# A graph layer's type embedding as one product of one-hot rows, its last 128 columns in two-relation chunks, and query units moved behind the second query tile

## The chip, the cores and the metric

The kernel runs on one core of a Trainium2 chip. The metric is the device time of one execution in microseconds (us); lower is better. PE is TensorE (PEld its weight loads), DVE is VectorE, ACT is ScalarE, POOL is GpSimd, SP is the engine that issues most DMAs.

## What is computed

The input `x` has 625 nodes of 768 features; there are 10,000 edges with a relation of 0 to 2, and each node has a type of 0 to 2. Two blocks follow one another, each `x + gnn + attention`, then `x + feed-forward`. The change lies in the first block. Its graph part is three relational layers:

```python
def rgcn_conv(h, src, dst, edge_type, w_rel, w_root, bias):
    xw = einsum('nd,rde->rne', h, w_rel)
    msg = xw[edge_type, src] * inv[dst, edge_type][:, None]   # inv: 1 / edges of that relation at dst
    return segment_sum(msg, dst) + h @ w_root + bias

h = concatenate([xn, node_emb[node_type]], axis=-1)     # 768 + 128 = 896 features
h = relu(rgcn_conv(h, ..., w_rel1, w_root1, b1))        # 896 -> 896
h = relu(rgcn_conv(h, ..., w_rel2, w_root2, b2))        # 896 -> 768
h = relu(rgcn_conv(h, ..., w_rel3, w_root3, b3))        # 768 -> 768
```

`xn` is the normalised `x`; `node_emb` is 3 x 128. The attention beside it has 12 heads of 64 with 256 random features, `relu` of the features of queries and keys, and no softmax.

## The kernel before

All matrix products run on PE with operands split in two: `hi` is the value rounded to the type PE takes, `lo` the rest, and a product is hi*hi + hi*lo + lo*hi, three matmuls (`split_product`, L179; `split_product_wide`, L187, with two halves of 314 nodes as the moving side, six matmuls). The 625 nodes are five tiles (`TT`), the last of 113; 896 features are seven slabs of 128 (`K1`), 768 are six (`KD`).

**Weights** come through a ring of two slots (`Ring`, `Stream`). A chunk is up to seven slabs by 256 columns. SP loads chunk n as soon as DVE has split chunk n-2 (`load_chunk`, L102); ACT writes `hi` (`ring_high`, L128) once PE is done with chunk n-2 (`st.freed`), then DVE writes `lo` (`ring_low`, L139), and PE waits for that (`st.split`).

**The stages that matter here** run one after another, with a barrier between:

- `phase_attend` "m0", six head pairs. For a pair PE makes key features of five tiles (`features_k`, L476), four tiles of query features m = 0 to 3 (`features_q`, L502), the products of keys and values (`keys_values`, L526) and the attention output. The next pair's key and query projections are cut in 12 units of six matmuls (`project_unit`, L187), and strewn in between: one after each key tile and one more, one after each of the query tiles 0, 1 and 2, and three behind `keys_values`. ACT copies a query tile (L645), DVE writes its low part (`pq_lo`, L771); query tile m waits for `pq_lo` of tile m-2, whose PSUM banks it takes.
- `phase_project` "p0": the attention's output projection (15 tiles, L179), while DVE and ACT decode packed edge counts. Here the type embedding is made: `embedding_rows` builds one-hot rows (L1016 to L1019), `embed` multiplies by them on PE (L905), ACT and DVE write the result and its low part as `k.et`, a seventh slab beside the six of `k.xt`. Then a check of the counts (L914) and a short loop that recounts.
- `phase_rgcn` "g1", the first layer (896 to 896), and "g2". The output columns are cut by 256, with 128 left over in g1: cuts 0 to 3. A written-out list of jobs sets the order on all engines:

```python
jobs = [(kind, c, r) for c in range(len(cuts))
        for kind, r in (("Y", 0), ("Y", 1), ("G", 0), ("Y", 2), ("G", 1), ("R", 3), ("G", 2))]
```

"Y r" is h times the weights of relation r: five tiles in PSUM banks 0 to 2 in turn, 7 x 3 matmuls each; ACT (L1503) and DVE (L1536) write the two halves of `y`. Tile i waits for `y_lo` of tile i-3. "G r" multiplies `y` by the edge counts (L1479, 20 matmuls of 314 columns for 128 output columns), "R" is h times the root weights, transposed (L187, 42 matmuls of 314 for 128 output columns). DVE adds G and R up. Each job uses one chunk of weights but G, which uses none.

In g1 the reciprocals of the counts are made first: PE sums counts (`sum_counts`, L1442; relations 0 and 1 ahead of all jobs, 2 behind tile 4), and DVE runs `inverse` six times, each behind a `y_lo` (`INVERSE_AT`, tiles 0, 1, 2, 3, 6, 7; L1520, L1521, L1524, L1525). The first "G" waits until the last of them has read its sums (`sum_read`, set by L1521).

Of the kernel before, what the change touches and what calls it, by code (L numbers as in the profile page):

```python
# [6 lines left out]
F32 = mybir.dt.float32  # L7
# [10 lines left out]
P = 128  # L18
# [150 lines left out]
def rgcn_chunks(w_rel, w_root):  # L169

    d_in, d_out = w_root.shape
    return [(d_in // P, w, [(0, w, weight_view(m)[:, :, c:c + w])])
            for c, w in column_cuts(d_out) for m in (w_rel[0], w_rel[1], w_rel[2], w_root)]
# [161 lines left out]
def phase_attend(k, name, second, rf=None):  # L335
# [3 lines left out]
    with ExitStack() as ctx:  # L339
# [87 lines left out]
        def _(pe):  # L427
# [54 lines left out]
            def features_q(p):  # L482
                for m in range(4):
# [29 lines left out]
                    if m < 3:  # L513
                        project_unit(p + 1, KD + m)

# [289 lines left out]
EMBED_AT = 7  # L805
PROJ_BANKS = 4
# [3 lines left out]
def phase_project(k, name, src, dst, edge_type, node_emb, node_type):  # L810
# [13 lines left out]
    with ExitStack() as ctx:  # L824
# [25 lines left out]
        type_i = spare[0:RELS, part[6]].bitcast(I32)[:, 0:NODES]  # L850
        type_f = spare[0:RELS, part[7]][:, 0:NODES]
        onehot = spare[0:RELS, part[8]]
# [3 lines left out]
            "edges_loaded", "emb_loaded", "iota_made", "own_made", "emb_made", "emb_ready", "emb_hi", "emb_lo",  # L856
# [13 lines left out]
        def _(sp):  # L870
# [30 lines left out]
        def _(pe):  # L901
            def embed():
                pe.wait_ge(s["emb_made"], 1)
                for h in range(2):
                    mm = pe.matmul(k.pair[3][:, h, 0:HN], emb_sb[:], onehot[:, h * HN:(h + 1) * HN], start=True, stop=True)  # L905
                mm.then_inc(s["emb_ready"], 1)

            def check():
# [8 lines left out]
                pe.wait_ge(s["emb_lo"], 1)  # L917
                pe.matmul(k.banks[7][:, 0:2], k.ones[:], over[:], start=True, stop=True).then_inc(s["check_mm"], 1)

            for c in range(3):  # L920
                pe.wait_ge(*st.split(c))
                wh = st.views(c)
                for t in range(TT):
# [10 lines left out]
                    if i == EMBED_AT:  # L934
                        embed()
# [16 lines left out]
        def _(act):  # L952
# [7 lines left out]
            for t in range(TT):  # L960
# [12 lines left out]
                if t == 3:  # L973
                    act.wait_ge(s["emb_ready"], 1)
                    act.activation(halves(k.et[:, 0, 0, :]), k.pair[3][:, :, 0:HN], ACT.Copy).then_inc(s["emb_hi"], 1)
# [3 lines left out]
        def _(dve):  # L979
# [77 lines left out]
            dve.memset(quot[:, 0, 0:P], 1.0).then_inc(s["ones_f"], 1)  # L1057
            dve.memset(shift[:], -(BASE / 2 - 1) / BASE).then_inc(s["shift_made"], 1)
# [5 lines left out]
            for i in range(3 * TT):  # L1064
# [10 lines left out]
                if i == EMBED_AT - 3:  # L1075
                    embedding_rows()
# [297 lines left out]

RECOUNT = 2
STEPS = RELS * ET // RECOUNT


def phase_rgcn(k, name, h_in, h_out, d_in, d_out, bias, layer):
# [5 lines left out]
    cuts = column_cuts(d_out)  # L1385
    with ExitStack() as ctx:  # L1386
# [9 lines left out]
            "sum_mm", "sum_read"))  # L1396
# [4 lines left out]
        jobs = [(kind, c, r) for c in range(len(cuts))  # L1401
# [1643 lines left out]
```

## Time and profile before

| | us |
|---|---|
| median of 3 runs (lowest, highest) | 2229.34 (2228.92, 2235.43) |
| the profiled execution | 2230.74 |
| its span, first to last instruction | 2229.0 |

| stage | from, to in the span (us) |
|---|---|
| attention m0, from its first product | 62.4 to 261.4 |
| projection p0 | 261.4 to 316.3 |
| first relational layer g1 | 316.3 to 579.1 |
| second and third layer | 579.1 to 981.7 |
| feed-forward, second block | 981.7 to 2229.0 |

PE is busy for 91% of the span. In the timeline a row is one instruction, or some like ones in a run; its length of 0.28 us for a matmul is that from first column in to last out, and the pace is the distance of two starts. In brackets stands how long the engine was idle, and who ended that.

### The profile page before, as it was taken

What the parts mean: (1) busy time and instruction counts of PE and PEld (TensorE: products, weight loads), DVE (VectorE), ACT (ScalarE), POOL (GpSimd) and SP (SyncE); (2) the same over time, 40 slices, a digit from 0 to 9 for tenths busy, and PEclk for the clock granted to TensorE, in tenths of its full rate; (3) what the DMA queues carried; (4) which work ended last, traced back from release to release, by engine and by line L of the source; (5) the groups of instructions that cost most, each with busy time, mean ns of one, the idle gap of its engine ahead of it and who ended that gap; (6) DMA issues with size and microseconds to landing.
All of it is one profiled execution on the core that took longest, in us unless ns stands there. A gap on an engine that the chain in (4) does not pass through costs nothing. (4 is left out here: it accounts for less than half of the span.)

```text
span 2229.0 us, 34175 instructions
## 1 busy us (share of the span) xinstructions
PE 2031.5 (91%) x13715; PEld 1919.2 (86%) x13715; DVE 1324.0 (59%) x1860; ACT 940.3 (42%) x1143; POOL 89.9 (4%) x70
## 2 busy tenths in 40 slices
PE   5899889999999999955899979799979999999996
PEld 4889779999999999955789879699968888888885
DVE  8455665333334343446456756553358888888886
ACT  6444411221211122111356633222247777777775
POOL 0000000000000000000001100000000100101001
PEclk9999989999999999977899978899989999999998
DMA  3311134211111121110210030412269999999997
GB/s 81 101 29 29 57 100 93 67 34 51 51 58 58 29 73 49 58 29 1 93 29 29 15 135 15 158 48 93 79 233 385 384 384 378 366 372 374 367 374 269
DMA packets 186156, 313.71 MB, mean 141 GB/s; under 512 B 12641, under 2 KB 86884, under 8 KB 185628
## 3 DMA queue, kind: packets, MB, share of 16 engines
q1 hardware_dynamic: 180956, 295.38, 38.0%
q0 software_dynamic: 4816, 16.62, 3.2%
q8 instruction: 88, 1.44, 0.3%
q14 instruction: 24, 0.20, 0.0%
q10 hardware_dynamic: 272, 0.07, 0.0%
HBM read 293.56 MB, written 20.40 MB: 141 GB/s over the span
## 5 line engine op out<-in xcount | busy, mean ns | idle before, releaser
L179 PE MATMUL psum<-re_whi,xt_sb 128*128 128x512 f32 (+1 forms) x1680 | 507.5, 377 | 1.5 <-DVE xt_sb L2794 1.5
L179 PE MATMUL psum<-ring_hi,xt_sb 128*128 128x256 f32 (+3 forms) x1980 | 369.1, 284 | 10.8 <-DVE m_v L694 3.9
L179 PEld LDWEIGHTS psum<-re_whi,xt_sb 128*128 128x128 f32 x1680 | 313.0, 189 | 47.0 <-issue 1.9
L2778 DVE TENSOR_TENSOR re_wlo<-moe_raw,re_whi 128x1536 fp32r<-128x1536 f32 x173 | 303.5, 1756 | 35.1 <-ACT re_whi L2732 34.4
L179 PEld LDWEIGHTS psum<-ring_hi,xt_sb 128*128 128x128 f32 (+1 forms) x1980 | 312.0, 190 | 12.0 <-issue 5.3
L179 PE MATMUL psum<-re_wlo,xt_sb 128*128 128x512 f32 (+1 forms) x840 | 313.2, 373 | 0.0
L2732 ACT ACTIVATE re_whi<-moe_raw 128x1536 fp32r<-128x1536 f32 x174 | 258.7, 1490 | 90.7 <-PE psum L179 86.7
L179 PE MATMUL psum<-ring_lo,xt_sb 128*128 128x256 f32 (+3 forms) x990 | 280.5, 283 | 0.0
L179 PEld LDWEIGHTS psum<-ring_lo,xt_sb 128*128 128x128 f32 (+1 forms) x990 | 188.1, 190 | 0.0
L179 PEld LDWEIGHTS psum<-re_wlo,xt_sb 128*128 128x128 f32 x840 | 158.9, 189 | 22.1
L128 ACT ACTIVATE ring_hi<-ring_raw 128x1536 fp32r<-128x1536 f32 (+2 forms) x67 | 102.2, 1526 | 159.8 <-PE psum L187 81.3
L2778 DVE TENSOR_TENSOR re_wlo<-re_more,re_whi 128x1536 fp32r<-128x1536 f32 x84 | 147.6, 1758 | 29.7 <-ACT re_whi L2732 29.7
L179 PE MATMUL psum<-ring_hi,gnn_sb 128*128 128x256 f32 (+1 forms) x810 | 150.1, 286 | 6.9 <-PEq L1386 4.2
L139 DVE TENSOR_TENSOR ring_lo<-ring_raw,ring_hi 128x1536 fp32r<-128x1536 f32 (+2 forms) x67 | 121.5, 1813 | 56.2 <-ACT ring_hi L128 56.0
L2732 ACT ACTIVATE re_whi<-re_more 128x1536 fp32r<-128x1536 f32 x84 | 125.2, 1490 | 41.4 <-PE psum L179 37.6
L1536 DVE TENSOR_TENSOR g_y<-psum,g_y 128x256 fp32r<-128x256 f32 (+3 forms) x105 | 42.4, 405 | 168.7 <-ACT g_y L1503 168.5
L187 PE MATMUL psum<-xt_sb,ring_hi 128*128 128x314 f32 x744 | 140.2, 310 | 0.0
L1503 ACT ACTIVATE g_y<-psum 128x256 fp32r<-128x256 f32 (+3 forms) x105 | 38.7, 369 | 232.9 <-PE psum L179 232.9
L179 PEld LDWEIGHTS psum<-ring_hi,gnn_sb 128*128 128x128 f32 (+1 forms) x810 | 127.5, 190 | 8.1 <-issue 7.8
L1479 PE MATMUL psum<-gnn_sb,g_y 128*128 128x314 f32 (+1 forms) x780 | 117.1, 308 | 0.0
L187 PEld LDWEIGHTS psum<-xt_sb,ring_hi 128*128 128x128 f32 x744 | 115.7, 191 | 0.0
L179 PE MATMUL psum<-ring_lo,gnn_sb 128*128 128x256 f32 (+1 forms) x405 | 115.6, 285 | 0.0
(400 smaller groups left out, 3288.5 us busy)
## 6 DMA issues: line engine op xcount, KB each, us to landing
moe_raw<-in_L_ffn_Wg_r SPq DMA_DIRECT2D x74, 768.0 KB, 9.0
moe_raw<-in_L_ffn_Wu_r SPq DMA_DIRECT2D x58, 768.0 KB, 8.4
moe_raw<-in_L_ffn_Wd_r SPq DMA_DIRECT2D x42, 768.0 KB, 6.2
re_more<-in_L_ffn_Wd_r SPq DMA_DIRECT2D x42, 768.0 KB, 9.4
re_more<-in_L_ffn_Wu_r SPq DMA_DIRECT2D x30, 768.0 KB, 7.8
ring_raw<-in_L_gnn_w_rel SPq DMA_DIRECT2D x18, 896.0 KB, 5.1
re_more<-in_L_ffn_Wg_r SPq DMA_DIRECT2D x15, 768.0 KB, 7.3
ring_raw<-in_L_mix_W_qkv SPq DMA_DIRECT2D x24, 384.0 KB, 4.4
```

The source lines that it names most:

```text
L128: act.activation(ring.hi[:, g % RING_SLOTS, 0:size], ring.raw[:, g % RING_SLOTS, 0:size], ACT.Copy).then_inc(ring.hi_done, 1)
L139: dve.tensor_tensor(lo, raw, hi.bitcast(F32), ALU.subtract).then_inc(ring.lo_done, 1)
L179: mm = pe.matmul(out, lhs[a], rhs[b], start=(first and i == 0), stop=(last and i == 2))
L187: mm = pe.matmul(bank_pair[:, h, 0:HN], lhs[a], rhs(b, h), start=(first and i == 0), stop=(last and i == 2))
L1479: mm = pe.matmul(pair[:, h, 0:HN], y[0:TS[t], v % 2, t, a, m * P:(m + 1) * P], k.C[0:TS[t], r, t, h * HN:(h + 1) * HN], start=(t == 0 and ...
L1503: act.activation(y[0:TS[t], v % 2, t, 0, 0:w], k.banks[i % 3][0:TS[t], 0:w], ACT.Copy).then_inc(s["y_hi"], 1)
L1536: dve.tensor_tensor(y[0:TS[t], v % 2, t, 1, 0:w], k.banks[i % 3][0:TS[t], 0:w], y[0:TS[t], v % 2, t, 0, 0:w].bitcast(F32), ALU.subtract).t ...
L2732: act.activation(whi[:, slot, :], raw[i % RAWS], ACT.Copy).then_inc(s["hi_done"], 1)
L2778: dve.tensor_tensor(wlo[:, i % RING, :], raw[i % RAWS], whi[:, i % RING, :].bitcast(F32), ALU.subtract)\
```

## The change

- **Embedding.** `k.et` is gone. p0 now makes `k.kind_rows` (99 used rows by 628 columns: a one-hot column of three types, four times over, at rows 0, 32, 64 and 96) and `k.emb` (the embedding turned, 128 by 35: hi in columns 0 to 2, lo in 32 to 34); the PE product `embed` is gone from it. In g1, `embed_products(n)` multiplies `k.emb` by the seventh slab of chunk n, hi and lo (two matmuls, 35 x 256, bank 3); ACT (`embed_high`) and DVE (`embed_low`) write its halves into `ew`; and each output tile gets, in place of three products with the seventh slab, one with `kind_rows` and `ew`, which waits for `ew_lo`. `embed_products` of the next chunk stands behind tile 3 of a Y job, or behind the first half of R, and waits for that chunk's split; that of chunk 0 stands ahead of everything.
- **Last cut of g1.** Its chunks are relations 0 and 1 side by side, and relation 2 beside the root. "Y 0" makes both relations' `y` at 256 columns, "Y 1" is gone, and the order is Y 0, Y 2, G 0, G 1, R, G 2. Chunks of g1: 14 for 16.
- **Attention m0.** The three query units of the next pair all stand behind query tile 1. In the second block's attention they stay.

```diff
 def rgcn_chunks(w_rel, w_root):
+    sides, chunks = (w_rel[0], w_rel[1], w_rel[2], w_root), []
+    for c, w in column_cuts(d_out):
+        for group in (sides[0:2], sides[2:4]) if w == P else [(m,) for m in sides]:
+            chunks.append((d_in // P, w * len(group),
+                           [(w * i, w * (i + 1), weight_view(m)[:, :, c:c + w]) for i, m in enumerate(group)]))
...
# features_q, phase_attend
-                    if m < 3:
+                    if second and m < 3:
                         project_unit(p + 1, KD + m)
+                    elif m == 1:
+                        for u in range(KD, KD + 3):
+                            project_unit(p + 1, u)
...
# phase_project
-            sp.dma_start(emb_sb[:], node_emb).then_inc(s["emb_loaded"], 16)
+            sp.dma_start(emb_f[:], node_emb.rearrange("r e -> e r"), allow_slow_non_contiguous=True).then_inc(s["emb_loaded"], 16)
...
-            for r in range(RELS):
-                sp.dma_start(type_i[r:r + 1, :], node_type.rearrange("(a n) -> a n", a=1)).then_inc(s["emb_loaded"], 16)
+            sp.dma_start(type_i, node_type.partition_broadcast(P)).then_inc(s["types_loaded"], 16)
...
-                    if i == EMBED_AT:
-                        embed()
...
# rgcn_plan, the order of jobs
+        order = (("Y", 0), ("Y", 2), ("G", 0), ("G", 1), ("R", 3), ("G", 2)) if w == P else \
+            (("Y", 0), ("Y", 1), ("G", 0), ("Y", 2), ("G", 1), ("R", 3), ("G", 2))
...
# phase_rgcn, tensor
+            def embed_products(n):
+                w = st.chunks[n][1]
+                pe.wait_ge(*st.split(n))
+                if n >= 1:
+                    pe.wait_ge(s["ew_lo"], n)
+                for a, v in enumerate(st.views(n)):
+                    mm = pe.matmul(k.banks[3][0:EMB_ROWS, 0:w], k.emb[:], v[:, KD, :], start=(a == 0), stop=(a == 1))
+                mm.then_inc(s["ew_mm"], 1)
...
+            if layer == 0:
+                embed_products(0)
                 sum_counts(0)
                 sum_counts(1)
...
-                        for j in range(kt):
+                        for j in range(full):
                             mm = split_product(pe, k.banks[i % 3][0:TS[t], 0:w],
...
+                        if layer == 0:
+                            pe.wait_ge(s["ew_lo"], n + 1)
+                            mm = pe.matmul(k.banks[i % 3][0:TS[t], 0:w], k.kind_rows[0:TYPE_ROWS, t * P:t * P + TS[t]],
+                                           ew[0:TYPE_ROWS, n % 2, off:off + w], start=False, stop=True)
                         mm.then_inc(s["y_mm"], 1)
+                        if t == EMBED_TILE and job in begins:
+                            embed_products(begins[job])
...
# phase_rgcn, vector
+            def embed_low(n):
+                w = st.chunks[n][1]
+                dve.wait_ge(s["ew_hi"], n + 1)
+                dve.tensor_tensor(ew[64:TYPE_ROWS, n % 2, 0:w], k.banks[3][0:EMB_ROWS, 0:w],
+                                  ew[0:EMB_ROWS, n % 2, 0:w].bitcast(F32), ALU.subtract).then_inc(s["ew_lo"], 1)
...
+            if layer == 0:
+                dve.memset(ew[:].bitcast(F32), 0.0).then_inc(s["ew_zero"], 1)
+                embed_low(0)
             ring_low(dve, st, 1)
```

`full` is 6 in g1 (7 slabs before) and stays `kt` elsewhere; `ew` has two slots of 256 columns.

The order of instructions at three places. First PE in m0, query tiles 1 to 3 of a pair that has a next one (L502, now L506, is a query tile; L187, now L191, a unit of `xt_sb`; names in brackets are the semaphores waited for). Before:

```order
L502 MATMUL psum<-m_qk,m_rf 128x314 [waits m0_pk_lo]
L502 MATMUL psum<-m_qk,m_rf 128x314 x3
L187 MATMUL psum<-xt_sb,ring_hi 128x314 x4
L187 MATMUL psum<-xt_sb,ring_lo 128x314 x2
L502 MATMUL psum<-m_qk,m_rf 128x314 [waits m0_pq_lo]
L502 MATMUL psum<-m_qk,m_rf 128x314 x3
L187 MATMUL psum<-xt_sb,ring_hi 128x314 x4
L187 MATMUL psum<-xt_sb,ring_lo 128x314 x2
L502 MATMUL psum<-m_qk,m_rf 128x314 [waits m0_pq_lo]
L502 MATMUL psum<-m_qk,m_rf 128x314 x3
L526 MATMUL psum<-m_v,m_phik 128x130 [waits m0_qk_lo,m0_pk_lo]
```

and now:

```order
L506 MATMUL psum<-m_qk,m_rf 128x314 [waits m0_pk_lo]
L506 MATMUL psum<-m_qk,m_rf 128x314 x3
L191 MATMUL psum<-xt_sb,ring_hi 128x314 x4
L191 MATMUL psum<-xt_sb,ring_lo 128x314 x2
L191 MATMUL psum<-xt_sb,ring_hi 128x314 x4
L191 MATMUL psum<-xt_sb,ring_lo 128x314 x2
L191 MATMUL psum<-xt_sb,ring_hi 128x314 x4
L191 MATMUL psum<-xt_sb,ring_lo 128x314 x2
L506 MATMUL psum<-m_qk,m_rf 128x314 [waits m0_pq_lo]
L506 MATMUL psum<-m_qk,m_rf 128x314 x3
L506 MATMUL psum<-m_qk,m_rf 128x314 [waits m0_pq_lo]
L506 MATMUL psum<-m_qk,m_rf 128x314 x3
```

Two units (12 matmuls) have moved ahead of query tile 2, and nothing stands between tiles 2 and 3 and `keys_values`.

Second PE in g1, last cut, a tile's end and the next one's start (`xt_sb` and `et_sb` are the features, `ring` the weights, `types_sb` is `kind_rows`, `emb_sb` is `k.emb`). Before, relation 0 alone:

```order
L179 MATMUL psum<-ring_lo,xt_sb 128x128
L179 MATMUL psum<-ring_hi,xt_sb 128x128
L179 MATMUL psum<-ring_hi,et_sb 128x128
L179 MATMUL psum<-ring_lo,et_sb 128x128
L179 MATMUL psum<-ring_hi,et_sb 128x128
```

and now relations 0 and 1 together, between tiles 3 and 4:

```order
L183 MATMUL psum<-ring_hi,xt_sb 128x256
L1516 MATMUL psum<-g_ew,types_sb 128x256
L1492 MATMUL psum<-ring_hi,emb_sb 35x256
L1492 MATMUL psum<-ring_lo,emb_sb 35x256
L183 MATMUL psum<-ring_hi,xt_sb 113x256
L183 MATMUL psum<-ring_lo,xt_sb 113x256
```

Three products with the seventh slab became one with the type rows, the width is 256, and two products of 35 rows for the next chunk follow.

Third DVE in g1, behind tile 3 of the first Y job (L1536, now L1625, is `y_lo`). Before:

```order
L1536 TENSOR_TENSOR g_y<-psum,g_y 128x256
L1520 TENSOR_SCALAR g_pos<-psum 128x314
L1521 TENSOR_SCALAR g_cnt<-psum 128x314
L1524 RECIPROCAL g_cnt<-g_cnt 128x314
L1525 TENSOR_TENSOR a_sb<-g_cnt,g_pos 128x314
L1536 TENSOR_TENSOR g_y<-psum,g_y 113x256
```

and now:

```order
L1625 TENSOR_TENSOR g_y<-psum,g_y 128x256
L1610 TENSOR_TENSOR g_ew<-psum,g_ew 35x256
L1600 TENSOR_SCALAR g_pos<-psum 128x314
L1601 TENSOR_SCALAR g_cnt<-psum 128x314
L1604 RECIPROCAL g_cnt<-g_cnt 128x314
L1605 TENSOR_TENSOR a_sb<-g_cnt,g_pos 128x314
L1625 TENSOR_TENSOR g_y<-psum,g_y 113x256
```

`embed_low` stands between `y_lo` of tile 3 and the fourth `inverse`, so all that follows comes after it.

## Rows read from the trace of the kernel before

**Rows 1.** The page, section 1: busy us, share of the span and instructions by engine.

```profile
PE 2031.5 (91%) x13715; PEld 1919.2 (86%) x13715; DVE 1324.0 (59%) x1860; ACT 940.3 (42%) x1143; POOL 89.9 (4%) x70
```

**Rows 2.** Busy time by engine in three stages; columns: stretch, length, PE, PEld, DVE, ACT, POOL, PEclk, DMA, GB/s.

```profile
62.38:261.39 199.01, 179.61 (x1304) 175.88 (x1305) 102.10 (x150) 83.95 (x130) 0.13 (x1) 0.97 0.16 45
261.39:316.29 54.90, 45.25 (x328) 41.40 (x328) 40.59 (x87) 15.23 (x20) 0.66 (x1) 0.90 0.26 80
316.29:579.14 262.85, 258.37 (x2005) 257.93 (x2005) 114.02 (x156) 49.14 (x84) 3.80 (x3) 0.99 0.25 68
```

**Rows 3.** The same view for four jobs of the first relational layer.

```profile
421.86:434.44 12.58, 12.58 (x108) 12.58 (x106) 2.51 (x5) 1.54 (x4) 0.00 (x0) 1.00 0.21 70
440.29:452.55 12.26, 12.26 (x87) 12.26 (x85) 2.49 (x3) 0.00 (x0) 0.00 (x0) 1.00 0.22 73
525.54:548.41 22.87, 22.87 (x212) 22.87 (x211) 7.27 (x15) 4.19 (x12) 0.00 (x0) 1.00 0.14 42
551.37:562.78 11.41, 11.41 (x108) 11.41 (x106) 1.98 (x5) 1.11 (x4) 0.00 (x0) 1.00 0.26 82
```

**Rows 4.** Timeline of PE, query features of one pair (start, length, engine, line, operation, count).

```profile
171.90 0.75 PE L187 MATMUL psum<-xt_sb,ring_hi 128*128 128x314 f32 x4
...
174.33 0.85 PE L502 MATMUL psum<-m_qk,m_rf 128*128 128x314 f32 x4 [1.38 <-DVE m_phiq L771]
...
175.88 0.75 PE L502 MATMUL psum<-m_qk,m_rf 128*128 128x314 f32 x4
176.47 0.23 PE L526 MATMUL psum<-m_v,m_phik 128*128 128x130 f32 x1
```

**Rows 5.** Timeline of DVE, the same place.

```profile
171.67 1.76 DVE L720 SCALAR_TENSOR_TENSOR m_qk<-psum,qk_bias,m_qk 64x628 fp32r<-64x628 f32 x2 [2.03 <-ACT m_qk L589]
173.46 1.53 DVE L771 SCALAR_TENSOR_TENSOR m_phiq<-psum,m_phiq 128x628 fp32r<-128x628 f32 x2
```

**Rows 6.** Timelines of DVE and PE, start of the attention output of the pair before.

```profile
157.93 0.69 DVE L791 TENSOR_TENSOR m_kv<-m_kvf,m_kv 128x512 fp32r<-128x512 f32 x1 [0.70 <-ACT m_kv L657]
...
158.72 0.51 PE L187 MATMUL psum<-m_phiq,m_kv 128*128 128x314 f32 x2
```

**Rows 7.** Timeline of PE, projection stage, around the embedding product.

```profile
280.34 1.32 PE L905 MATMUL psum<-a_sb,node_emb 3*128 3x314 f32 x4
281.59 0.39 PE L179 MATMUL psum<-ring_hi,gnn_sb 128*128 128x256 f32 x1
```

**Rows 8.** Timeline of PE, start of the first relational layer.

```profile
316.29 5.57 PE L1442 MATMUL psum<-gnn_sb,ones_r 128*128 128x314 f32 x20 [4.61 <-PEq L824]
321.66 0.41 PE L179 MATMUL psum<-ring_hi,xt_sb 128*128 128x256 f32 x1
321.87 0.41 PE L179 MATMUL psum<-ring_lo,xt_sb 128*128 128x256 f32 x1
```

**Rows 9.** Timeline of DVE, first two Y jobs of that layer.

```profile
336.93 0.42 DVE L1536 TENSOR_TENSOR g_y<-psum,g_y 128x256 fp32r<-128x256 f32 x1
337.27 0.47 DVE L1520 TENSOR_SCALAR g_pos<-psum 128x314 f32<-128x314 f32 x1
...
340.85 0.42 DVE L1536 TENSOR_TENSOR g_y<-psum,g_y 113x256 fp32r<-113x256 f32 x1
...
348.09 0.47 DVE L1521 TENSOR_SCALAR g_cnt<-psum 128x314 f32<-128x314 f32 x1
```

**Rows 10.** Timeline of PE, the same stretch.

```profile
341.33 0.39 PE L179 MATMUL psum<-ring_hi,xt_sb 128*128 128x256 f32 x1 [0.27 <-DVE g_y L1536]
...
348.88 0.60 PE L1479 MATMUL psum<-gnn_sb,g_y 128*128 128x314 f32 x3
```

**Rows 11.** Timeline of DVE, second cut, the split behind its Y 0.

```profile
405.83 2.03 DVE L139 TENSOR_TENSOR ring_lo<-ring_raw,ring_hi 128x1792 fp32r<-128x1792 f32 x1 [1.17 <-ACT ring_hi L128]
```

**Rows 12.** Timeline of PE, second cut, end of tile 3 of Y 1.

```profile
413.44 0.28 PE L179 MATMUL psum<-ring_hi,et_sb 128*128 128x256 f32 x1
413.56 0.28 PE L179 MATMUL psum<-ring_hi,xt_sb 128*113 128x256 f32 x1
```

More of the change, by code:

```diff
@@ L901, in _ @@
         def _(pe):
[L902 to L906, printed above, removed]
             def check():
@@ L1408, in phase_rgcn, with width @@
                 g_count += cuts[c][1] // P
+        y_read = {}
+        for (c, r), (v, _) in y_of.items():
+            y_read[v] = max(y_read.get(v, 0), g_at[c, r] + cuts[c][1] // P)
+            st.freed[chunk_of[c, r][0]] = (s["y_mm"], TT * (v + 1))
         for c in range(len(cuts)):
-            for r in range(RELS):
-                st.freed[4 * c + r] = (s["y_mm"], TT * (y_at[c, r] + 1))
-            st.freed[4 * c + 3] = (s["g_mm"], g_at[c, 3] + cuts[c][1] // P)
+            st.freed[chunk_of[c, RELS][0]] = (s["g_mm"], g_at[c, RELS] + cuts[c][1] // P)
+        begins, seen = {}, set()
+        for job in jobs:
+            n = chunk_of[job[1], job[2]][0]
+            if job[0] != "G" and n not in seen:
+                seen.add(n)
+                if layer == 0 and n + 1 < len(st.chunks):
+                    begins[job] = n + 1
+        ends = {chunk_of[c, r][0]: (kind, c, r) for kind, c, r in jobs if kind != "G"}
+        splits = {job: n + RING_SLOTS for n, job in ends.items() if n + RING_SLOTS <= len(st.chunks)}
         block = ctx.enter_context(k.nc.Block())
+        def width(c, r):
+            return cuts[c][1] * len(y_jobs[y_of[c, r][0]][1])
         @block.sync
@@ L1465, in _ @@
                     continue
-                for m in range(w // P):
+                for m in range(cuts[c][1] // P):
                     i = g_at[c, r] + m
@@ L1488, in _, with embed_high @@
                     mm.then_inc(s["g_mm"], 1)
+                    if kind == "R" and m == 0 and job in begins:
+                        embed_products(begins[job])
         @block.scalar
         def _(act):
+            def embed_high(n):
+                w = st.chunks[n][1]
+                if n == 0:
+                    act.wait_ge(s["ew_zero"], 1)
+                if n >= 2:
+                    act.wait_ge(*st.freed[n - 2])
+                act.wait_ge(s["ew_mm"], n + 1)
+                act.activation(ew[0:EMB_ROWS, n % 2, 0:w], k.banks[3][0:EMB_ROWS, 0:w], ACT.Copy).then_inc(s["ew_hi"], 1)
@@ L1503, in _ @@
                         act.activation(y[0:TS[t], v % 2, t, 0, 0:w], k.banks[i % 3][0:TS[t], 0:w], ACT.Copy).then_inc(s["y_hi"], 1)
-                if kind != "G" and 4 * c + r + RING_SLOTS <= len(st.chunks):
-                    ring_high(act, st, 4 * c + r + RING_SLOTS)
+                        if t == EMBED_TILE and job in begins:
+                            embed_high(begins[job])
+                elif kind == "R" and job in begins:
+                    embed_high(begins[job])
+                if job in splits:
+                    ring_high(act, st, splits[job])
                 if kind == "G" and r == 2:
-                    for m in range(w // P):
+                    for m in range(cuts[c][1] // P):
                         i = 2 * c + m
@@ L1560, in _ @@
                         dve.wait_ge(s["g_read"], i + 1)
-                    if kind == "R" and m == w // P - 1 and 4 * c + r + RING_SLOTS <= len(st.chunks):
-                        ring_low(dve, st, 4 * c + r + RING_SLOTS)
+                    if m == 0 and job in begins:
+                        embed_low(begins[job])
+                    if m == ms - 1 and job in splits:
+                        ring_low(dve, st, splits[job])
                     if kind == "G" and r == 2:
                         dve.tensor_scalar(sum_, sum_, 0.0, None, ALU.max).then_inc(s["h_f"], 1)
-                        if m == w // P - 1:
-                            for m2 in range(w // P):
+                        if m == ms - 1:
+                            for m2 in range(ms):
                                 o = 2 * c + m2
```

137 lines of the change are left out of this document (86 added, 51 removed).

## The prediction

> **What bounds the kernel now.** I read the page first: PE is busy for 2031.5 of 2229 us [rows 1]. Then the stages, where its granted clock is 0.90 to 0.99: in g1 PE is busy 258.4 of 262.9 us and DVE 114.0, so a product less is time less; m0 has 19 us of idle PE (199.0 less 179.6), and p0 some 10 [rows 2]. Then single jobs, where PE is busy end to end [rows 3]; the first two columns of such a row are all that counts here, since its product count also takes in neighbours at the edges (105, 84, 210 for two jobs in one, and 105 are theirs by the code). Last the timelines at the three places whose order changes. All of the change lies before 579 us; what follows it is the same program, and I count it as unchanged.
>
> **Pace of PE.** A Y job of 256 columns is 105 products in 12.58 us, 0.120 us each; R is 84 of 314 columns in 12.26 us, 0.146 each; at 128 columns 210 take 22.87 us and 105 take 11.41, 0.109 each [rows 3]. So a product of half the width costs nine tenths of a whole one. The Trainium skill ("TensorE: Matmul & The Clock Gate", section "Back-to-back issue gap") speaks against the merged cut: it has 81 ns for a sustained product of 128 columns, and N/2.4 + 2.5 ns, 109 ns at 256, for a single one. By that the merged job would save 210 x 0.081 - 95 x 0.109 = 6.7 us in place of the 11.5 below, as an estimate from that page; the rows have 0.109 and 0.120, and I go by them.
>
> **Attention m0.** Now query tile 2 waits for DVE: PE idles 1.38 us until `pq_lo` of tile 0 [rows 4], since DVE first writes the low part of the next keys (L720 from 171.67) and then that of tile 0 from 173.46, two of them in 1.53 us, so the first is done near 174.27 [rows 5]. That time does not hang on where query units stand. Tile 2 starts at 174.33, one unit and tile 3 follow at 175.88, `keys_values` at 176.47 [rows 4]. With all three units behind tile 1, PE still waits for the same low part, but has 0.87 us less to do behind it: 1.55 us without a start (172.78, which is 171.90 + 6 x 0.146, to 174.33) become about 0.7, and tile 3 starts once tile 2 is through and the second low part is there, both near 175.05. So `keys_values` starts 0.82 us earlier. Behind it the attention output waits for a chain of ACT and DVE that begins at the end of `keys_values` and moves with it; in the pair before, its last step ends at 158.62, and the output starts at 158.72, behind 18 products of units [rows 6]. Five pairs have a next one: 5 x 0.82 = **-4.1 us**. Bounds: 0, should that chain come out late by as much, and -6.9, all of 5 x 1.38.
>
> **Projection p0.** `embed` goes: four PE records from 280.34 to the next product at 281.59 [rows 7], **-1.25 us**. DVE loses a memset, and a low part of 628 columns shrinks to three; it gains a few operations of one to three columns ahead of its first low part, which waits for ACT anyway. Bounds: 0 (DVE's decoding sets the time of the check instead) and -1.5. The turned embedding comes by 384 packets of four bytes and the types by 320 KB in place of 7.5; both are wanted 7 us or more behind their issue, so I cost them at nothing. If either were late, DVE's decoding and with it the check would be late.
>
> **g1, up to the first G.** Here the gain is lost. PE gets 2 products first, at the low clock that stands behind the barrier (sum products 0.27 us apart in the row: 5.37 us for 20; the first Y products 0.21) [rows 8]: +0.5 us. Its tile 0 then ends about when it does now, since it has two products less. From there DVE sets the pace: a `y_lo` and an `inverse` take 3.9 us, from 336.93 to 340.85 [rows 9], for each of the first four tiles, where a tile of PE is 2.5 (12.58 / 5 [rows 3]) and will be 2.3. Already now tile 7 starts only at 341.33, released by DVE, and G 0 starts at 348.88 [rows 10] while the last L1521, on which it depends, runs from 348.09 for 0.47 us, to 348.56 [rows 9]. So PE has 0.3 us to spare there and would be 1.4 us ahead after the change. But DVE gets `embed_low` before the fourth `inverse`: near 0.35 us (a 256-column subtract is 0.42 and the next starts 0.34 on [rows 9]), and its chain starts 0.1 us later. L1521 ends near 349.0, and G 0 starts near 349.1: **+0.2 us** where the products alone would give -1.4. PE then waits in tile 5 for `ew_lo` (some 0.5 us) and before tile 7 (about 1.5 us for 0.43 now). Bounds: -1.4, and +2.5 (below).
>
> **g1, the rest.** Seven more full-width Y jobs lose 10 products each (21 to 19 a tile, five tiles): 7 x 10 x 0.120 = **-8.4 us**. R loses 4 of 42 for each 128 columns, seven times: 28 x 0.146 = **-4.1 us**. The last cut's Y jobs are 22.87 + 11.41 = 34.28 us [rows 3] and become 95 products of 256, 95 x 0.120 = 11.4, and 95 of 128, 95 x 0.109 = 10.3: **-12.6 us**. Eleven embedding steps remain behind the first G, two products each: 22 x 0.120 = **+2.6 us**; I take the 256-column pace for them and for the kind product, although one has 35 output rows and the other 99 input rows, since no row shows such shapes; bounds are 0.109 and 0.146, which is -0.2 to +0.6 us for the 22 and -0.4 to +1.0 for the 40 kind products of 256 columns behind the first G. The chain from product to `ew_lo` is about 0.4 + 0.4 us of ACT and DVE and some 0.3 between; the next chunk's first kind product comes at least one tile and 18 products later (over 4 us), so it is hidden. The split is now wanted earlier: in Y 1 behind tile 3 and not, as for its first use now, behind a G. In the second cut the split for it ends at 407.86 [rows 11], while tile 3 ends at 413.56 [rows 12], or 1.0 us less when tiles are shorter: 4.7 us of slack, and the loads are issued a whole job ahead. Every other chunk has a G or half an R more.
>
> **Sum.** -4.1 - 1.25 + 0.2 - 8.4 - 4.1 - 12.6 + 2.6 = **-27.65 us**. Against the profiled execution, 2230.74 (its span of 2229.0 and 1.7 around it, which I leave as it is), that is 2203.1; against the median of the three runs, which is 1.4 us lower, **2201.7**. A difference of 0.3%, 6.7 us, is about what a measurement of this kernel can tell from none.
>
> **Rivals.**
> 1. *m0 gives nothing.* The chain behind `keys_values` (ACT's copy, DVE's sum, ACT, DVE) competes with the ring split that DVE and ACT run there, and the attention output waits as long as it gained. For it: the margin is 0.1 us [rows 6]. Against: the split starts behind the last query tile and moves along. Then 2205.8.
> 2. *A bubble at each kind product.* It waits for `ew_lo` in the middle of a tile, and its weight load can't run ahead. The Trainium skill ("TensorE: Matmul & The Clock Gate", "Architectural detail: the array is 16× 32×32, not 1× 128×128") says that PE's queue pulls weight loads ahead of products in flight; it doesn't say that a wait hinders that. There are 55 + 7 such waits; at 0.11 us each (a product's spacing) they cost 6.8 us: 2208.5. Against it: the first product of tile 4 also stands behind a wait, and follows the last of tile 3 by 0.12 us like any other [rows 12].
> 3. *The clock falls in g1's first cut.* PE idles 1.5 us there, in place of 0.4. In m0 idle times of 1.38 us leave the clock at full speed in the stage's mean of 0.97 [rows 2, 4]. Should it fall, products at 0.21 us and not 0.12 for 3 us cost some 2 us: 2204; this is the +2.5 bound.
> 4. *Slower: splits too late.* If each embedding step waited for its chunk's split, PE would stand still in order. To lose 27.65 us over 13 steps it takes 2.1 us each, hence, with the slack of 4.7, splits 6.8 us later than now. Should they be 10 us later, the price is 13 x 5.3 = 69 less 27.65: 2270. Nothing in the rows points that way, since a split is 2.03 us on DVE [rows 11].
> 5. *It doesn't do what it says,* the removed products being hidden behind something: excluded by PE's 258.4 of 262.9 us [rows 2] for g1, but for its first cut, as costed.
>
> **Chances.** The forecast, within about 2.5 us of the sum: 0.66. Rival 1 in whole or half: 0.14. Rival 2: 0.07. Rival 3: 0.06. Rival 4: 0.02. No change, by a mix: 0.01. More gain than forecast (m0's bound, a quicker start of g1): 0.04. Rivals 1 and 3 are inside the range, and most of rival 2; the range is 2197 to 2209. Faster by over 0.3%: 0.97; within: 0.01; slower: 0.02.
>
> **What would show it.** m0: idle time before query tile 2 near 0.6 us and 24.0 us a pair (24.8 now); else that step is wrong. p0: no L905-like product and the stage 1.2 us shorter. g1: G 0 starts 32.8 us behind the stage's first product (now 348.88 - 316.29 = 32.6); PE idle before tile 7 near 1.5 us; a full-width Y job 11.4 us, and 0.24 more with its embedding step; R 11.1 us; last cut's Y jobs 11.4 and 10.3 us; the stage near 240.6 us for 262.9. Idle time of PE before L1516, beyond tile 5 of the first cut, or before L1492 would prove the hidden chain wrong, and a changed stage behind g1 would prove wrong that the rest stays as it is.

## The result, and the profile after

The changed kernel takes 2202.76 us, the median of four runs (2194.82 to 2204.11), against 2230.61 for four of the kernel before: a ratio of 0.9864 with a 95% interval of 0.9836 to 0.9893, 27.85 us less. The forecast was 2201.7 us against the median before, and 2203.1 for the profiled execution, which took 2203.24 us with a span of 2201.5. Whether the terms held is a question of its own. The page's first section, where PE has 24.9 us less than in [rows 1]:

```profile
PE 2006.6 (91%) x13496; PEld 1892.4 (86%) x13496; DVE 1327.5 (60%) x1873; ACT 942.4 (43%) x1150; POOL 90.6 (4%) x70
```

The window view of the changed kernel for m0, p0 and g1 (columns as in [rows 2]):

```profile
61.95:259.03 197.08, 182.46 (x1305) 177.92 (x1305) 101.73 (x153) 83.94 (x130) 0.14 (x1) 0.96 0.16 45
259.03:313.73 54.70, 45.06 (x323) 42.12 (x324) 40.02 (x89) 14.60 (x19) 0.67 (x1) 0.87 0.28 85
313.73:552.10 238.37, 232.32 (x1790) 231.16 (x1790) 119.21 (x164) 52.38 (x91) 3.80 (x3) 0.99 0.28 75
```

Against [rows 2] m0 is 1.9 us shorter (4.1 was forecast), p0 0.2 (1.25) and g1 24.5 (22.3). So the sum hit, and three terms missed. The same view for four jobs of g1 that answer to [rows 3]: Y 1 of the third cut, its R with an embedding step, and the last cut's two Y jobs (the first with its step):

```profile
457.71:468.92 11.21, 11.21 (x98) 11.20 (x97) 4.48 (x7) 3.76 (x7) 0.00 (x0) 1.00 0.30 83
494.46:505.79 11.33, 11.33 (x81) 11.29 (x79) 2.93 (x5) 0.38 (x1) 0.00 (x0) 1.00 0.23 76
511.64:523.07 11.43, 11.43 (x99) 11.41 (x98) 5.87 (x11) 3.18 (x7) 0.00 (x0) 1.00 0.23 75
523.07:533.40 10.33, 10.33 (x98) 10.33 (x96) 3.52 (x6) 3.08 (x6) 0.00 (x0) 1.00 0.00 0
```

A full-width Y job is 11.2 us for 12.4 to 12.6, R is 11.33 - 0.24 = 11.1 for 12.26, and the last cut has 11.43 - 0.24 + 10.33 = 21.5 us for 34.28: as forecast. The timeline of PE behind tile 3 of the first Y job:

```profile
326.97 0.28 PE L1516 MATMUL psum<-g_ew,types_sb 99*128 99x256 f32 x1
327.09 0.28 PE L1492 MATMUL psum<-ring_hi,emb_sb 128*35 128x256 f32 x1
327.21 0.28 PE L1492 MATMUL psum<-ring_lo,emb_sb 128*35 128x256 f32 x1
327.33 0.28 PE L183 MATMUL psum<-ring_hi,xt_sb 128*113 128x256 f32 x1
```

The product with the type rows (99 rows in; the "kind product" of the prediction), the two of the embedding step (35 out) and an ordinary one (113 out) start 0.12 us apart. There is no bubble at the wait, where `ew_lo` is there in time; rival 2 falls here.

Timeline of PE in m0, answering to [rows 4]:

```profile
172.38 0.46 PE L191 MATMUL psum<-xt_sb,ring_lo 128*128 128x314 f32 x2
173.35 1.57 PE L506 MATMUL psum<-m_qk,m_rf 128*128 128x314 f32 x8 [0.51 <-DVE m_phiq L778]
174.75 0.45 PE L533 MATMUL psum<-m_v,m_phik 128*128 128x130 f32 x3
```

Relative to the pair's first key features (161.29; 162.27 before), tile 2 starts at 12.06 us in both kernels, to the hundredth: its release by DVE doesn't hang on the units. `keys_values` starts at 13.46 for 14.20, 0.74 us earlier. Timeline of PE in g1's first cut, tile 5's last product, tile 7's first, and G 0; then DVE's `embed_low(1)` and its last read of the sums (answering to [rows 8 to 10]):

```profile
333.72 0.39 PE L1516 MATMUL psum<-g_ew,types_sb 99*128 99x256 f32 x1 [0.41 <-DVE g_ew L1610]
...
337.76 0.38 PE L183 MATMUL psum<-ring_hi,xt_sb 128*128 128x256 f32 x1 [1.40 <-DVE g_y L1625]
...
345.05 0.41 PE L1537 MATMUL psum<-gnn_sb,g_y 128*128 128x314 f32 x1
```

```profile
333.25 0.42 DVE L1610 TENSOR_TENSOR g_ew<-psum,g_ew 35x256 fp32r<-35x256 f32 x1
...
344.52 0.47 DVE L1601 TENSOR_SCALAR g_cnt<-psum 128x314 f32<-128x314 f32 x1
```

All three are the places named in the forecast, and DVE is what PE waits for: 0.41 us for `ew_lo`, 1.40 before tile 7, and G 0 0.06 us behind the last L1601 (344.52 + 0.47). But G 0 starts 31.32 us behind the stage's first product, 313.73, and not 32.8.

### The profile page after: what moved, and what is told of

Same layout as the page of the kernel before. It is cut to its first block and busy times, and to the rows that moved or that the text cites. A ratio compares the mean times of both kernels' runs of the same rounds, so it can differ in the third digit from the quotient of the medians.

```text
span 2201.5 us, 33777 instructions
## 1 busy us (share of the span) xinstructions
PE 2006.6 (91%) x13496; PEld 1892.4 (86%) x13496; DVE 1327.5 (60%) x1873; ACT 942.4 (43%) x1150; POOL 90.6 (4%) x70
## 3 DMA queue, kind: packets, MB, share of 16 engines
q8 instruction: 86, 1.41, 0.3%
## 5 line engine op out<-in xcount | busy, mean ns | idle before, releaser
L183 PE MATMUL psum<-ring_hi,xt_sb 128*128 128x256 f32 (+3 forms) x1920 | 357.5, 285 | 11.9 <-DVE m_v L701 3.9
L183 PEld LDWEIGHTS psum<-ring_hi,xt_sb 128*128 128x128 f32 (+1 forms) x1920 | 302.7, 190 | 13.1 <-issue 5.2
L183 PE MATMUL psum<-ring_lo,xt_sb 128*128 128x256 f32 (+3 forms) x960 | 272.5, 284 | 0.0
L183 PEld LDWEIGHTS psum<-ring_lo,xt_sb 128*128 128x128 f32 (+1 forms) x960 | 182.4, 190 | 0.0
L139 DVE TENSOR_TENSOR ring_lo<-ring_raw,ring_hi 128x1536 fp32r<-128x1536 f32 (+1 forms) x65 | 121.2, 1864 | 55.9 <-ACT ring_hi L128 55.8
L128 ACT ACTIVATE ring_hi<-ring_raw 128x1536 fp32r<-128x1536 f32 (+1 forms) x65 | 101.8, 1567 | 98.1 <-PE psum L183 44.5
L191 PE MATMUL psum<-xt_sb,ring_hi 128*128 128x314 f32 x744 | 139.8, 310 | 0.0
L1625 DVE TENSOR_TENSOR g_y<-psum,g_y 128x256 fp32r<-128x256 f32 (+3 forms) x100 | 41.6, 417 | 140.6 <-ACT g_y L1579 140.3
L191 PEld LDWEIGHTS psum<-xt_sb,ring_hi 128*128 128x128 f32 x744 | 115.3, 190 | 0.0
```

What stands on the lines that cost most here:

```text
L128: act.activation(ring.hi[:, g % RING_SLOTS, 0:size], ring.raw[:, g % RING_SLOTS, 0:size], ACT.Copy).then_inc(ring.hi_done, 1)
L139: dve.tensor_tensor(lo, raw, hi.bitcast(F32), ALU.subtract).then_inc(ring.lo_done, 1)
L183: mm = pe.matmul(out, lhs[a], rhs[b], start=(first and i == 0), stop=(last and i == 2))
L191: mm = pe.matmul(bank_pair[:, h, 0:HN], lhs[a], rhs(b, h), start=(first and i == 0), stop=(last and i == 2))
L1625: dve.tensor_tensor(y[0:TS[t], v % 2, t, 1, 0:w], k.banks[i % 3][0:TS[t], 0:w], y[0:TS[t], v % 2, t, 0, 0:w].bitcast(F32), ALU.subtract).t ...
```

## Experiments

Eleven runs, each beside the kernel before on the same chip (two of them repeat the changed kernel and the kernel before); "low clock" is time in which the trace's record of the granted clock has 0.5, 1.2 GHz (for a window row about twice what PEclk lacks to 1, times its length). With executions of one kernel that differ by up to 14 us, medians alone can't settle terms of 1 to 4 us, so each verdict rests on the length of the stage concerned. Ratios in brackets are to the kernel before, with the 95% interval.

**The changed kernel again.**

> The changed kernel once more, as the base for the runs beside it. Theory A (the terms of the sum are fixed costs): the stages keep their lengths of the first profile within 0.3 us: m0 196.65, p0 54.7, first relational layer 238.4. Theory B (what m0 and p0 gave was partly hidden, and the first relational layer's start partly favoured, by where the granted clock stood at 1.2 GHz): these three lengths change by 0.5 to 1.5 us between profiles of the same kernel, in step with how long the granted clock stands at 0.5 in each, while a steady pair of m0 stays at 24.08 us and the stretch behind the first G at 207.05 us. Time near 2203 under both.

2200.52 us (0.9858, 0.9835 to 0.9880). Window view: last pair of m0, p0 up to its last projection product, g1 up to G 0.

```profile
233.46:264.88 31.42, 23.62 (x103) 21.72 (x101) 9.01 (x20) 9.71 (x17) 0.14 (x1) 0.62 0.02 3
```

```profile
318.03:350.36 32.33, 30.48 (x226) 29.78 (x227) 26.32 (x36) 7.57 (x14) 3.80 (x3) 0.92 0.85 196
264.88:303.03 38.15, 38.15 (x300) 37.97 (x301) 32.61 (x67) 14.61 (x19) 0.67 (x1) 0.96 0.41 122
```

Behind G 0 the rest of g1 is 207.05 us, exactly as in the first profile, and pairs are 24.07 to 24.10. The other lengths moved as theory B says, in step with low clock, and one of them by more than its 1.5 us: m0's last pair is 31.42 us with 23.9 us of low clock, where the first profile had 25.49 with 7.3; p0's products 38.2 for 39.4, with 3.4 us of low clock for 6.3; g1 up to G 0 32.33 for 31.32, with 5.1 for 2.8. Theory A falls; theory B holds but for the size in m0.

**Only the query units.** The kernel before, with

```diff
-                    if m < 3:
+                    if second and m < 3:
                         project_unit(p + 1, KD + m)
+                    elif m == 1:
+                        for u in range(KD, KD + 3):
+                            project_unit(p + 1, u)
```

> The kernel before with the query units moved and nothing else. Theory A (DVE's low part of tile 0 is what query tile 2 waits for, and its time doesn't hang on the units): a steady pair takes 24.05 to 24.1 us for 24.8, the idle time before tile 2 is near 0.5 us for 1.38, and the kernel is 3.7 to 4.1 us faster than the kernel before. Rival (the attention output's chain of ACT and DVE comes late by as much): pairs stay at 24.8, 0 us. Rival (the gain in the changed kernel came with the rest of the change): 0 us too.

2227.19 us for 2230.76 (0.9976, 0.9963 to 0.9990), 3.6 us less by medians, 5 by the ratio. Window view, one steady pair, and g1 up to G 0:

```profile
137.03:161.09 24.06, 23.54 (x174) 23.12 (x173) 13.80 (x19) 11.93 (x18) 0.00 (x0) 1.00 0.12 33
```

```profile
314.55:346.68 32.13, 31.82 (x240) 31.61 (x241) 25.16 (x33) 6.72 (x11) 3.80 (x3) 0.92 0.88 202
```

A pair is 24.06 us (24.8 before), the five together 124.2 for 127.95. The gain is m0's own, and rival 1 of the prediction falls.

**The last cut taken apart.** The changed kernel, with

```diff
-        for group in (sides[0:2], sides[2:4]) if w == P else [(m,) for m in sides]:
+        for group in [(m,) for m in sides]:
```

and the plan of jobs to match.

> The changed kernel with the last 128 columns in four chunks of one relation each, as before, so only the merging is undone. Theory A (a product costs 0.109 us at 128 columns and 0.118 at 256, as the rows show): three Y jobs of 95 x 0.109 = 10.35 us take the place of 11.2 and 10.3, and two more embedding steps of 128 columns come: slower than the changed kernel by 9.5 + 0.4 = 9.9 us. Theory C (sustained products of 128 columns cost 0.081 us when issued without gaps, by the page named in the prediction): slower by about 5 us. Rival D (a chunk of two relations brings its own costs, such as a later split or G jobs that wait): slower by less than 9.

2207.81 us (0.9899, 0.9877 to 0.9920), 7.3 us over the changed kernel by medians, 9 by the ratios. The stretch from G 0 to the end of g1, in this kernel and in the changed one:

```profile
344.98:561.62 216.64, 212.42 (x1663) 211.97 (x1663) 94.60 (x138) 45.98 (x86) 0.00 (x0) 1.00 0.18 54
```

```profile
345.05:552.10 207.05, 202.84 (x1564) 202.37 (x1564) 92.90 (x129) 44.81 (x77) 0.00 (x0) 1.00 0.19 56
```

9.59 us: theory A. Three jobs of 95 products at 128 columns take 10.3 us each, 0.109 us a product, as the mean of four tiles of 128 rows and one of 113. The Trainium skill ("TensorE: Matmul & The Clock Gate", "Back-to-back issue gap") has 81 ns for it; in these products (fp32 data) the measurement decides against it. Timeline of PE, where shorter spacings stand, at an embedding step:

```profile
530.29 0.27 PE L1515 MATMUL psum<-g_ew,types_sb 99*128 99x128 f32 x1
530.40 0.23 PE L1491 MATMUL psum<-ring_hi,emb_sb 128*35 128x128 f32 x1
530.47 0.22 PE L1491 MATMUL psum<-ring_lo,emb_sb 128*35 128x128 f32 x1
530.53 0.26 PE L183 MATMUL psum<-ring_hi,xt_sb 128*113 128x128 f32 x1
530.63 0.26 PE L183 MATMUL psum<-ring_lo,xt_sb 128*113 128x128 f32 x1
```

Behind a product of 128 columns the next one starts after 0.06 to 0.07 us if it had 35 output rows, 0.10 if 113, 0.11 if 128. At 256 columns 35 and 128 rows cost the same 0.12.

**Only the embedding.** The changed kernel with both undone: query units strewn as before, last cut in four chunks.

> The embedding part of the change alone: type rows in place of a seventh slab, with the last cut in four chunks and the query units where they were. Theory A (the terms add): 27.85 less 3.7 for m0 and 9.9 for the merging leaves 14.2 us faster than the kernel before; by the terms of the prediction 1.25 + 8.4 + 4.1 + 1.1 (10 products of 0.109 for the 128-column Y job that the merging did not touch) + 2 x 1.1, less 0.2 and 3.0, is 13.9. Rival (a bubble of 0.11 us at each kind product, hidden in the whole by something else): about 7.

2216.81 us for 2230.78 (0.9946, 0.9929 to 0.9962): 14.0 us less by medians, 12 by the ratio. G 0 to the end of g1 is 216.64 us, as in the kernel above. The parts add (14.0 here, 3.6 of the query units and 9.6 of the merging are 27.2 us, for 27.85 of the whole), and a gain of about 7, as by the rival, is excluded.

**A product back in p0.** The changed kernel, with `emb_sb` loaded as before and, behind the eighth tile of the projection,

```diff
+            def embed():
+                pe.wait_ge(s["emb_loaded"], 32)
+                for h in range(2):
+                    pe.matmul(k.pair[3][:, h, 0:HN], emb_sb[:], k.xt[0:RELS, 0, 0, h * HN:(h + 1) * HN].bitcast(F32),
+                              start=True, stop=True)
```

> The changed kernel with a product like the removed one put back at its place in the projection stage (3 rows in, 128 out, twice 314 columns in full precision; its result is used by nobody). Theory A (the product's 1.25 us lay on PE's path, and the projection stage came out only 0.2 us shorter because its clock was low for longer): at equal time of low clock the stage's products take 1.25 us more, and the kernel is 1.2 us slower. Rival (DVE's decoding sets the end of the stage, and the product was hidden): 0 us, with idle time of PE before the check shorter by 1.25.

2200.56 us (0.9863, 0.9848 to 0.9877): in the executions' times the difference can't be seen. Timeline at the place, and the window up to the last projection product:

```profile
282.47 1.32 PE L913 MATMUL psum<-xt_sb,node_emb 3*128 3x314 f32 x4
283.73 0.38 PE L183 MATMUL psum<-ring_hi,gnn_sb 128*128 128x256 f32 x1
```

```profile
263.53:303.11 39.58, 39.58 (x305) 38.75 (x305) 32.62 (x67) 14.64 (x19) 0.67 (x1) 0.96 0.38 118
```

The record is that of [rows 7], and the stretch takes 39.58 us with 3.4 us of low clock. Sorted by low clock, the eleven profiles and the two first ones fall in place: with the product 39.55, 39.56 and 39.58 us at 3.1 to 3.4 us and 40.73 at 6.2; without it 38.11, 38.11 and 38.16 at 3.1 to 3.4, and 39.30 to 39.37 at 6.2 to 6.3. (Two more, of the kernels with fillers below, have 38.7 and 38.9 at 3.4: there the first products ran at full clock and waited for DVE.) So the product cost 1.4 us on PE's path, and 3 us more of low clock cost 1.2 and hid it in the first profile.

**The first reciprocal earlier.** The changed kernel, with

```diff
-INVERSE_AT = (0, 1, 2, 3, 6, 7)
+INVERSE_AT = (None, 0, 1, 2, 5, 6)
...
             dve.wait_ge(s["small"], 16)
+            if layer == 0:
+                inverse(0, 0)
```

> The changed kernel with the first reciprocal of the counts ahead of the first y_lo, where DVE stands idle for 2.6 us, and the others behind tiles 0, 1, 2, 5 and 6. Theory A (DVE's chain of low parts and reciprocals binds PE in the first cut): the waits in tile 5 (0.57 us over a product's spacing), before tile 7 (1.57) and before G 0 (0.17) go, 2.3 us faster than the changed kernel, and G 0 starts 2.3 us earlier behind the stage's first product. Rival (those idle times are borrowed: PE would wait later for the splits of the next chunks, for which DVE is late as well): less than 0.7 us. Slower, if tile 3 waits for a first y_lo that now comes 1 us later.

2198.08 us (0.9850, 0.9831 to 0.9869). Timeline of PE, the kind product of tile 5 and G 0:

```profile
332.66 0.39 PE L1516 MATMUL psum<-g_ew,types_sb 99*128 99x256 f32 x1 [1.31 <-DVE g_ew L1610]
...
342.10 0.60 PE L1537 MATMUL psum<-gnn_sb,g_y 128*128 128x314 f32 x3
```

G 0 comes 30.33 us behind the stage's first product (311.77), 1.0 us earlier at the same 2.8 us of low clock, not 2.3. The wait before tile 7 is gone, but tile 5 waits 1.31 us for `ew_lo`: I had put four reciprocals ahead of the low part of tile 3, where three were. DVE binds, as said; my order for it was a poor one. The last experiment has a better order.

**Low parts in halves.** The changed kernel, where `qk_high` signals behind each of its two copies in m0, and

```diff
-                dve.wait_ge(s["qk_hi"], qk_count(p, a))
                 for hd in range(2):
+                    dve.wait_ge(s["qk_hi"], 2 * qk_count(p, a) - 1 + hd)
```

(the lines for m0; in the second block's attention the one wait stays).

> The changed kernel, where in m0 DVE begins the low part of the next keys and queries behind the first of ACT's two copies and not behind both. Theory A (the rest of the wait before query tile 2 is DVE's chain behind ACT's copy of the keys, 1.57 us of ACT and 1.75 + 0.77 of DVE in a row): the chain ends 0.8 us earlier, the idle time before tile 2 (0.5 us in a pair, 0.7 start to start) goes, pairs take 23.4 us for 24.08, and the kernel is 5 x 0.67 = 3.3 us faster. Rival (keys_values, which waits for the same chain, or the attention output's chain takes the wait over): 0 to 1 us.

2191.69 us (0.9828, 0.9816 to 0.9841). Window view, one pair; timeline of PE at query tiles 2 and 3, and of DVE:

```profile
135.59:158.89 23.30, 23.30 (x174) 23.16 (x173) 13.81 (x18) 11.94 (x18) 0.00 (x0) 1.00 0.12 34
```

```profile
146.68 0.47 PE L191 MATMUL psum<-xt_sb,ring_lo 128*128 128x314 f32 x2
146.98 1.44 PE L506 MATMUL psum<-m_qk,m_rf 128*128 128x314 f32 x8
148.26 1.01 PE L533 MATMUL psum<-m_v,m_phik 128*128 128x130 f32 x8
```

```profile
144.20 1.75 DVE L732 SCALAR_TENSOR_TENSOR m_qk<-psum,qk_bias,m_qk 64x628 fp32r<-64x628 f32 x2 [1.24 <-ACT m_qk L596]
145.99 1.53 DVE L783 SCALAR_TENSOR_TENSOR m_phiq<-psum,m_phiq 128x628 fp32r<-128x628 f32 x2
```

A pair takes 23.30 us, PE is busy in all of it, and tile 2 follows the unit without a wait. DVE starts its part for the next keys 0.81 us behind ACT's start (144.20 behind 143.39), where it was 1.60. So it is in all three kernels with this edit; in the others with the moved units a pair takes 24.1. The five pairs together are 3.9 us shorter (120.35 for 124.25), for 3.3 expected. By the ratios the kernel is 6.7 us faster than the changed one; at most 3.9 of that are shown to be the edit's, and the intervals of the two ratios (3 and 5 us either way) allow for the rest.

**Both edits.**

> The changed kernel with both edits: first reciprocal ahead of the first y_lo, and DVE's low parts behind each half of ACT's copy. If the two theories hold the gains add: 2.3 + 3.3 = 5.6 us faster than the changed kernel, near 2197. If either wait is only moved, less by its part.

2193.01 us (0.9836, 0.9823 to 0.9849). Pairs of 23.3 us, G 0 at 30.40 us with 5.1 us of low clock (32.33 in the changed kernel at the same). The stages' gains add; that the median is 1.3 us above the last kernel's, and not below it, is within what executions differ by. With the first reciprocal moved, G 0 hardly hangs on low clock (30.33 us at 2.8, 30.40 at 5.1), where the changed kernel went from 31.32 to 32.33: at 5.1 us PE's slower products use up most of its wait in tile 5, which was 1.31 us in the first try and is 0.41 here. So the edit is worth 1.0 us at 2.8 us of low clock and 1.9 at 5.1.

**The kernel before again.** I suspected the moved units of the clock's fall in m0's last pair.

> The kernel before once more, for its profile: in the two profiles in which the query units are strewn as before, the last pair of m0 took 24.7 us and the granted clock fell there only behind keys_values; in the eight with all of them behind tile 1, it took 25.5 us (four times), 25.6, 29.8, 30.6 and 31.4, with 6.8 to 23.9 us at 1.2 GHz. Theory E (the last pair has no units, PE waits before every second tile, and the new timing of the pairs lets the clock fall early in it): 24.7 us again. Rival (it is chance, whatever the kernel): it may be 25.5 or more here too. The first relational layer up to the first G: 32.1 to 32.6 us, by the time at low clock in it.

2232.52 us for 2231.37 (1.0005, 0.9995 to 1.0016). Window view of the last pair, and PE's timeline there:

```profile
236.53:267.10 30.57, 22.10 (x102) 20.54 (x101) 8.82 (x17) 9.69 (x17) 0.13 (x1) 0.66 0.02 3
```

```profile
247.09 8.63 PE L526 MATMUL psum<-m_v,m_phik 128*128 128x130 f32 x40
...
258.16 6.21 PE L187 MATMUL psum<-m_phiq,m_kv 128*128 128x314 f32 x24 [2.44 <-DVE m_kv L791]
```

30.57 us at a mean clock of 0.66: theory E's second half falls. The clock falls early in the last pair (6.7 us into it) with the units strewn as before too, and in the kernel with both edits, whose units are moved, it fell only behind `keys_values` (15.5 us into it). But 24.7 us was seen in two of three profiles with strewn units and in none of eight with moved ones (25.5 at the least), so whether the moved units make the fall more likely stays open, as does what decides how long it lasts.

**Fillers in the last pair.** The changed kernel, with

```diff
+            def filler(p, n):
+                if second or p < PAIRS - 1:
+                    return
+                pe.wait_ge(s["qk_lo"], qk_count(p, QUERIES))
+                for _ in range(n):
+                    pe.matmul(qk_pair[QUERIES][:, 0, 0:HN], k.xt[:, 0, 0, 0:P], k.xt[:, 0, 0, 0:HN], start=True, stop=True)
```

> The changed kernel with filler products in the last pair of m0, whose result nobody uses: three of 314 columns behind key tiles 1 to 4 and query tiles 0 to 2, fourteen behind keys_values, so that PE is busy where it waited (0.4 to 0.5 us a tile, 2.45 us before the attention output). Theory E (PE's idle times in the last pair let its clock fall, and what the fall costs is 0.8 us in most executions and 5 to 7 in some): the granted clock stays at 2.4 GHz through the last pair, which takes 24.7 us, and the kernel is 1 to 4 us faster than the changed one. Rival (the clock falls for another reason, or the fillers delay the tiles): the fall stays and the pair takes 25.5 us or more, with the fillers' time on top where the clock is low.

2196.70 us (0.9845, 0.9831 to 0.9859), five runs from 2195.73 to 2199.64: by the ratios 2.9 us faster than the changed kernel, which the intervals don't tell from none. Window view of the last pair here, and in the first profile of the changed kernel; then PE's timeline from `keys_values` on:

```profile
232.72:255.88 23.16, 19.35 (x137) 17.68 (x136) 9.10 (x20) 9.73 (x17) 0.14 (x1) 1.00 0.02 4
```

```profile
233.54:259.03 25.49, 17.19 (x103) 15.47 (x101) 8.96 (x20) 9.71 (x17) 0.14 (x1) 0.86 0.03 4
```

```profile
242.36 4.58 PE L544 MATMUL psum<-m_v,m_phik 128*128 128x130 f32 x40
246.78 2.25 PE L466 MATMUL psum<-xt_sb 128*128 128x314 f32 x14
249.39 3.76 PE L191 MATMUL psum<-m_phiq,m_kv 128*128 128x314 f32 x24 [0.37 <-DVE m_kv L810]
```

The clock stays at 2.4 GHz, and the pair takes 23.16 us, less than the 24.67 of the best profile without fillers: with PE busy behind `keys_values`, the attention output takes 3.76 us (6.21 in the fence above, 5.28 in the first profiles). The first half of theory E holds: with PE's idle time in this pair filled, the clock stays up (in both profiles with fillers, and in none of the eleven without), and its fall costs 1.5 us at the least (24.67 - 23.16) and 8.3 at the most (31.42 - 23.16).

**All three.** Halves, fillers, and `INVERSE_AT = (None, 0, 1, 3, 5, 6)`.

> The changed kernel with DVE's low parts behind each half of ACT's copy, the fillers, and the reciprocals once more in another place: the first ahead of the first y_lo, the others behind tiles 0, 1, 3, 5 and 6, so that the low part of tile 3 and embed_low come one reciprocal earlier than in the first try, where tile 5 waited 1.31 us for ew_lo. If DVE's chain is what binds the first cut, G 0 now starts 29.0 to 29.3 us behind the stage's first product at 2.8 us of low clock (31.32 in the changed kernel, 30.33 in the first try), or 30.0 to 30.3 at 5.1 us. Steady pairs of m0 23.3 us, the last one 24.7 or less. Sum: 3.9 + 2.1 + 1 to 4, near 2193 us.

2188.76 us (0.9809, 0.9795 to 0.9823), runs from 2188.20 to 2191.46: the fastest kernel of the study, 42.6 us under the kernel before. Window view of the last pair and of g1 up to G 0:

```profile
228.60:251.76 23.16, 19.34 (x137) 17.68 (x136) 9.09 (x19) 9.73 (x17) 0.14 (x1) 1.00 0.03 5
305.97:336.18 30.21, 30.21 (x226) 29.91 (x227) 27.46 (x35) 7.57 (x14) 3.80 (x3) 0.91 0.85 212
```

In the first cut PE is busy in all of 30.21 us, with 5.6 us of low clock; the changed kernel needed 32.33 with 5.1. The 2.1 us or more are what was expected of DVE's chain. Most of it came with the first reciprocal's new place (30.40 at 5.1 us of low clock in the kernel with both edits); the better order took away the last wait, in tile 5.

## Why the prediction was right

The stages of the first two profiles, in us, and in the last column the difference where low clock was equal or the profiles agree (the last pair of m0 left out of its sum):

| | forecast | first profiles | at equal clock |
|---|---|---|---|
| up to the first key features of m0 | 0 | +0.52 | 0 |
| m0, five pairs with a next one | -4.1 | -3.70 | -3.7 |
| m0, last pair | 0 | +0.82 | open |
| p0 | -1.25 | -0.19 | -1.4 |
| g1 up to G 0 | +0.2 | -1.27 | +0.2 |
| g1 from G 0 | -22.5 | -23.21 | -23.2 |
| behind g1 | 0 | -0.45 | 0 |
| sum | -27.65 | -27.48 | -28.1 |

- **m0.** The mechanism was right and tile 2's time exact. The size, 0.82 a pair, was 0.74: tile 2 to `keys_values` is 1.40 us, where I had set tile 3 at 0.72 behind tile 2 and added the 0.6 of [rows 4].
- **p0.** The term was right within 0.15 us, in a stage that showed nothing of it. "The stage 1.2 us shorter" was a wrong test, since I gave the stage's low clock no room of its own.
- **g1 up to G 0.** "Here the gain is lost" holds: at 5.1 us of low clock it is 32.13 us with the embedding as before (only the query units moved) and 32.33 in the changed kernel, at 4.3 us 31.75 and 32.02. The 31.32 of the first profile came of a low clock of 2.8 us instead of 6.2; the sentence "PE gets 2 products first, at the low clock that stands behind the barrier" took that stretch's length for a constant.
- **g1 from G 0.** R, the last cut and the embedding steps were met within 0.2 us. The seven Y jobs gave 9.0 us and not 8.4: products now follow each other by 0.118 us, where they did by 0.119 before and the forecast had 0.120.
- **Rivals.** 1 and 2 fell to the pair's length and to the spacing at the kind product. 3: in the seven profiles that have the idle time before tile 7 (1.39 to 1.41 us) the clock stayed at full speed behind it. 4: no PE wait before an embedding step, but for the first, which opens the stage.
- **Sum.** The misses (+0.5, +0.4 and +0.8 up to the end of m0, +1.1 in p0, against -1.5 in g1's start, -0.7 behind it and -0.45 in the rest) nearly cancel. That the sum was met within 0.2 us is luck: by the last column the change is worth 28.1, less what the last pair may lose by it, and executions of one kernel differ by far more than either.

## What to carry to other kernels

Compare stages at equal granted clock before a term is called wrong: a low stretch behind a barrier can hide or feign a gain of 1 us. Where PE waits for a chain whose time doesn't hang on PE, move work from behind the wait to ahead of it; then shorten the chain, by signalling each half (0.8 us a pair here) or by starting it in idle time of its engine. Before moving a chain's links, write down for each consumer how many links now stand ahead of it.

## What was not expected of the hardware

- The time that the granted clock stays at 1.2 GHz differs between executions of one kernel: in m0's last pair 7.3, 20.5 and 23.9 us were seen in kernels that are the same there, for 25.5, 30.6 and 31.4 us. Fillers whose results nobody uses kept it at 2.4 GHz in both profiles that had them. The five runs of each of those two kernels spread by 3.9 and 3.3 us, the five runs of each of three kernels without them by 6.3 to 6.7, and nine of the changed kernel by 12.3; so few runs show no more than a hint.
- A narrow product's pace hangs on its output rows: at 128 columns 0.06 to 0.07 us with 35, 0.10 with 113, 0.11 with 128.
